# Attention graph units on one core: both column halves of a projection and all values in one round each, 71 rounds a unit

## What is computed

```python
for c in range(6):
    nsrc = min(c + 1, 5); snode = c - nsrc
    eq, ek, ev = lind + nsrc - 1, lind, lind + nsrc // 2
    q = ew[c, 0] * (nodes[c - 1] @ We[eq] + be[eq])
    k = ew[c, 1] * (nodes[snode] @ We[ek] + be[ek])
    v = ew[c, 2] * (nodes[snode + nsrc // 2] @ We[ev] + be[ev])
    o = mha(q, k, v, Wq[c], Wk[c], Wv[c], Wo[c])     # 8 heads of 16, softmax over 1024 keys
    nodes[c] = act_w[c] * o + q
    lind += nsrc
out = layernorm(nodes[5], ln_g, ln_b)
```

## Time and profile before

| what | value |
|---|---|
| median of three runs | 2990.59 us |
| the profiled execution: its time, its span | 2986.32 us, 2984.2 us |
| mean granted TensorE clock | 0.981 |
| TensorE matmul busy | 2845.6 us, 95% of the span |
| VectorE busy | 2396.8 us, 80% |
| ScalarE busy | 2163.1 us, 72% |
| GpSimd busy | 353.2 us, 12% |

### The profile page before, as it was taken

The page is one execution under the profiler, slowest core; times in us unless marked ns, Lnnn a source line. Parts: engine busy times, 40 slices in busy tenths (PEclk is TensorE's granted clock), DMA queues, the critical chain, the costliest instruction groups (busy, mean ns, idle before and its releaser), DMA issues. The chain is left out here.

```text
span 2984.2 us, 49063 instructions
## 1 busy us (share of the span) xinstructions
PE 2845.6 (95%) x18975; PEld 1281.3 (43%) x18975; DVE 2396.8 (80%) x3019; ACT 2163.1 (72%) x2738; POOL 353.2 (12%) x314
## 2 busy tenths in 40 slices
PE   7899999998689999999999999999999999999997
PEld 5566566555333333333333333333333333333332
DVE  6656656665778888888888888888888888888876
ACT  3455655565368888788888888888788888888777
POOL 0000000000001111111111111111111111111011
PEclk7899999999889999999999999999999999999999
DMA  6100000014424544544444534544544434544411
GB/s 149 38 9 12 19 11 14 3 44 80 81 72 84 105 100 96 112 102 88 100 100 96 115 98 84 108 99 96 115 100 87 103 99 94 117 101 92 85 64 40
DMA packets 146190, 239.49 MB, mean 80 GB/s; under 512 B 56802, under 2 KB 97142, under 8 KB 142630
## 3 DMA queue, kind: packets, MB, share of 16 engines
q1 hardware_dynamic: 145958, 236.36, 35.7%
HBM read 162.53 MB, written 70.98 MB: 78 GB/s over the span
## 5 line engine op out<-in xcount | busy, mean ns | idle before, releaser
L1747 ACT ACTIVATE pt_b<-ps_max 128x1024 f32<-128x1024 f32 x1514 | 1487.0, 1025 | 264.7 <-PE ps_max L1566 258.3
L1775 DVE TENSOR_REDUCE mx_b<-ps_pair 128x2 f32<-128x1024 f32 (+1 forms) x989 | 1195.6, 1209 | 176.0 <-PE ps_pair L1554 158.4
L1601 PE MATMUL ps_ctx<-pt_b,vs 128*32 128x512 f32 x6144 | 821.6, 607 | 2.6 <-ACT c_b L1730 2.6
L1775 DVE TENSOR_REDUCE mx_b<-ps_misc 128x1 f32<-128x512 f32 x989 | 673.2, 681 | 64.3 <-PE ps_misc L1554 59.5
L1566 PE MATMUL ps_max<-qs,ks 50*128 50x512 f32 x3028 | 688.9, 429 | 1.6 <-ACT part L1698 0.9
L1554 PE MATMUL ps_pair<-ks,qs 48*128 48x512 f32 x1955 | 490.6, 470 | 28.4 <-DVE mx_b L1775 24.5
L1566 PEld LDWEIGHTS ps_max<-qs,ks 50*128 50x128 f32 x3028 | 321.5, 186 | 257.3 <-ACT pt_b L1747 171.5
L1554 PE MATMUL ps_misc<-ks,qs 48*128 48x512 f32 x989 | 421.0, 426 | 5.0 <-DVE mx_b L1775 1.3
L1554 PEld LDWEIGHTS ps_pair<-ks,qs 48*128 48x128 f32 x1955 | 197.5, 184 | 519.2 <-DVE mx_b L1775 509.0
L931 ACT ACTIVATE pt<-ps_max,cb 128x512 f32<-128x512 f32 x340 | 215.3, 687 | 179.7 <-PE ps_max L658 117.2
L1554 PEld LDWEIGHTS ps_misc<-ks,qs 48*128 48x128 f32 x989 | 183.2, 185 | 212.2 <-DVE mx_b L1775 175.8
(11 more groups left out here) (216 smaller groups left out, 2250.0 us busy)
## 6 DMA issues: line engine op xcount, KB each, us to landing
partd<-part SPq DMA_DIRECT2D x22, 2048.0 KB, 9.1
qs<-partd SPq DMA_DIRECT2D x288, 128.0 KB, 5.6
ks<-partd SPq DMA_DIRECT2D x288, 128.0 KB, 6.6
xv<-node SPq DMA_DIRECT2D x26, 512.0 KB, 5.6
xf<-node SPq DMA_DIRECT2D x24, 512.0 KB, 4.6
xq<-node SPq DMA_DIRECT2D x23, 512.0 KB, 3.8
xk<-node SPq DMA_DIRECT2D x23, 512.0 KB, 4.7
rec_b<-invd SPq DMA_DIRECT2D x368, 32.0 KB, 1.8
```

The source lines that it names most:

```text
L1601: ins = pe.matmul(psO[SLOT * i:SLOT * i + SLOT, :], vs[u % 2][:, kb, QUAD * (s // HALF_STEPS) + i], pt[:, (QUAD * S + i) % ENTRIES], start ...
L1747: act.activation(pt[:, e:e + 2].rearrange("p k n -> p (k n)"), at[:], ACT.Exp, scale=SCALE_B).then_inc(exp_done, 1)
L1775: nc.vector.tensor_reduce(mx2[:, at:at + n], (psP, psX)[p % 2][:, 0:CHUNK * n].rearrange("p (h n) -> p h n", h=n), AX.X, ALU.max).then_inc ...
```

## The change

A project round now makes both halves: two matmuls of 512 columns fill both banks of its tile, and ScalarE copies 1024 columns at a time; there are two such rounds a unit (query, key). One values round makes all eight blocks of values, in both banks, and ScalarE copies them with two instructions. Counters of semaphores follow. `PLAN` has seven entries, so a steady unit has 71 rounds: turn 1 moves from round 6 to 2, the projections stand at 11 and 12 (before 11, 18, 23, 26), output 1 moves from 31 to 23, values stand at 34 (before 34, 39), turn 0 moves from 49 to 44. `PIECE_SLOT` is a new table for 142 slots. Unit 0 now has 70 rounds, so the table holds for units 1 to 21, and units 0 and 22 spread their pieces evenly.

```diff
-        PLAN = {6: ("turn", 0, 1), 9: ("output", -1, 0), 11: ("project", 2, 0), 18: ("project", 2, 1), 23: ("project", 2, 2), 26: ("project", 2, 3),
-                31: ("output", -1, 1), 34: ("values", 1, 0), 39: ("values", 1, 1), 49: ("turn", 1, 0)}
-        FIRST_PLAN = {**PLAN, 0: ("values", 0, 0), 1: ("values", 0, 1)}
+        PLAN = {2: ("turn", 0, 1), 9: ("output", -1, 0), 11: ("project", 2, 0), 12: ("project", 2, 1), 23: ("output", -1, 1),
+                34: ("values", 1, 0), 44: ("turn", 1, 0)}
+        FIRST_PLAN = {**PLAN, 0: ("values", 0, 0)}
...
-        PIECE_SLOT = (1, 2, 4, 7, 8, 10, 12, 14, 17, 18, 18, 19, 19, 24, 25, 27, 29, 30, 32, 33, 34, 36,
+        PIECE_SLOT = (0, 2, 4, 6, 9, 10, 12, 14, 15, 17, 19, 21, 21, 23, 23, 25, 27, 28, 28, 29, 31, 32,
...
-                    pe.matmul(to, wp[:, P * qk:P * qk + P], (xq, xk)[qk][:, CHUNK * c:CHUNK * c + CHUNK],
-                              start=True, stop=True).then_inc(pj_ready, 1)
...
+                    for c in range(NCHUNK):
+                        cols = slice(CHUNK * c, CHUNK * c + CHUNK)
+                        ins = pe.matmul(to[:, cols], wp[:, P * qk:P * qk + P], (xq, xk)[qk][:, cols], start=True, stop=True)
+                    ins.then_inc(pj_ready, 1)
...
+                    for kb in range(KB):
+                        ins = pe.matmul(to[:, P * kb:P * kb + P], xv[:, P * kb:P * kb + P], wv[:],
                                         start=True, stop=True)
...
-                    act.activation(full[:, qk, cols], at, ACT.Identity, bias=wp[:, 2 * P + qk:2 * P + qk + 1])
-                    act.activation(part[:, qk, 0, cols], at, ACT.Identity,
+                    act.activation(full[:, qk], at[:], ACT.Identity, bias=wp[:, 2 * P + qk:2 * P + qk + 1])
+                    act.activation(part[:, qk, 0], at[:], ACT.Identity,
...
-                        ins = act.activation(vs[w % 2][:, BPC * n:BPC * n + BPC, heads, DV * q:DV * q + DV],
-                                             at.rearrange("p (k h d) -> p k h d", k=BPC, h=HEADS)[:, :, heads],
+                        ins = act.activation(vs[w % 2][:, :, heads, DV * q:DV * q + DV],
+                                             at[:].rearrange("p (k h d) -> p k h d", k=KB, h=HEADS)[:, :, heads],
...
-                    pool.wait_ge(pj_copied, PJ * (w - 2) + n + 1)
+                    pool.wait_ge(pj_copied, 2 * (w - 2) + qk + 1)
```

More of the change, by code:

```diff
@@ L1517, in _, with project, values @@
             def _(pe):
-                def project(w, n, to):
-                    qk, c = n // NCHUNK, n % NCHUNK
-                    if n == 0:
+                def project(w, qk, to):
+                    if not qk:
                         pe.wait_ge(p_in, 3 * D16 * (w - 1))
-                    pe.matmul(to, wp[:, P * qk:P * qk + P], (xq, xk)[qk][:, CHUNK * c:CHUNK * c + CHUNK],
-                              start=True, stop=True).then_inc(pj_ready, 1)
-                def values(w, n, to):
-                    if n == 0:
-                        pe.wait_ge(v_in, 2 * D16 * (w + 1))
-                    for t in range(BPC):
-                        kb = BPC * n + t
-                        ins = pe.matmul(to[:, P * t:P * t + P], xv[:, P * kb:P * kb + P], wv[:],
+                    for c in range(NCHUNK):
+                        cols = slice(CHUNK * c, CHUNK * c + CHUNK)
+                        ins = pe.matmul(to[:, cols], wp[:, P * qk:P * qk + P], (xq, xk)[qk][:, cols], start=True, stop=True)
+                    ins.then_inc(pj_ready, 1)
+                def values(w, to):
+                    pe.wait_ge(v_in, 2 * D16 * (w + 1))
+                    for kb in range(KB):
+                        ins = pe.matmul(to[:, P * kb:P * kb + P], xv[:, P * kb:P * kb + P], wv[:],
                                         start=True, stop=True)
@@ L1663, in unit @@
                         elif kind == "values":
-                            values(w, k, to)
+                            values(w, to)
                         elif kind == "project":
-                            project(w, k, to[:, 0:CHUNK])
+                            project(w, k, to)
                         else:
@@ L1689, in _, with project, values @@
             def _(act):
-                def project(w, n, at):
-                    qk, c = n // NCHUNK, n % NCHUNK
-                    act.wait_ge(pj_ready, PJ * (w - 2) + n + 1)
-                    if n == 0 and w > 2:
+                def project(w, qk, at):
+                    act.wait_ge(pj_ready, 2 * (w - 2) + qk + 1)
+                    if not qk and w > 2:
                         act.wait_ge(spilled, D16 * (w - 2))
-                    cols = slice(CHUNK * c, CHUNK * c + CHUNK)
-                    act.activation(full[:, qk, cols], at, ACT.Identity, bias=wp[:, 2 * P + qk:2 * P + qk + 1])
-                    act.activation(part[:, qk, 0, cols], at, ACT.Identity,
+                    act.activation(full[:, qk], at[:], ACT.Identity, bias=wp[:, 2 * P + qk:2 * P + qk + 1])
+                    act.activation(part[:, qk, 0], at[:], ACT.Identity,
                                    bias=wp[:, 2 * P + qk:2 * P + qk + 1]).then_inc(pj_copied, 1)
-                def values(w, n, at):
-                    act.wait_ge(v_ready, 2 * w + n + 1)
+                def values(w, at):
+                    act.wait_ge(v_ready, w + 1)
                     for q in range(2):
                         heads = slice(QUAD * q, QUAD * q + QUAD)
-                        ins = act.activation(vs[w % 2][:, BPC * n:BPC * n + BPC, heads, DV * q:DV * q + DV],
-                                             at.rearrange("p (k h d) -> p k h d", k=BPC, h=HEADS)[:, :, heads],
+                        ins = act.activation(vs[w % 2][:, :, heads, DV * q:DV * q + DV],
+                                             at[:].rearrange("p (k h d) -> p k h d", k=KB, h=HEADS)[:, :, heads],
                                              ACT.Identity)
@@ L1751, in unit @@
                         elif kind == "values":
-                            values(w, k, at[:, 0:CHUNK])
+                            values(w, at)
                         elif kind == "project":
-                            project(w, k, at[:, 0:CHUNK])
+                            project(w, k, at)
                         else:
@@ L1822, in finish_sums @@
                     if k == 4:
-                        dve.wait_ge(v_ready, 2 * UNITS)
+                        dve.wait_ge(v_ready, UNITS)
                     elif k >= PARTS_Y - NCHUNK:
```

12 lines of the change are left out of this document (6 added, 6 removed), and 6 rows, old and new, of the table PIECE_SLOT.

## The result

The changed kernel takes 3057.80 us (median of 4 runs, 3054.96 to 3060.68), the kernel before 2986.02 beside it (4 runs, 2975.85 to 2990.75): a ratio of 1.0243, 95% interval 1.0221 to 1.0264. It is slower by 72 us. The forecast was 3055, slower, with a range of 3005 to 3085.

The account below looks back on a forecast made before the run. TensorE's order with its tile waits was taken as the bound. +3.3 us a unit gave +70 for units 1 to 21, unit 0 -4, unit 22 -1: +65 on 2986.3, 3051; the median's 4.3 made 3055, range 3005 to 3085.

Parts of the forecast that it names:

- Fewer breaks, projections, values: TensorE in a steady unit: four fewer runs -1.2 us, two double projections -0.4, one values round of eight -0.15.
- Tile waits: TensorE waits until VectorE has reduced a maxima tile; in longer runs 8.7 us a unit against 3.6, +5.1.
- P s x P: Run before projection 0: pair of maxima, two score matmuls, misc-tile single, pair; 2.25 us against 1.14, idle 0.9.
- p s x P: Run before the values: pair-tile single, two score matmuls, misc-tile single, pair of maxima; 1.70 us against 1.02.
- the 10: Unbroken run of ten score and maxima matmuls on TensorE: 2.70 us by a hand walk, 2.84 by the row kept.
- the combine: VectorE's combine of the halves at the unit's end, near GpSimd's product: taken at 0, bounds +4 and -7 us in all.
- ScalarE's copies: Eight projection copies of 512 columns (0.69 us each) become four of 1024 (1.02); costed at nothing.
- Moved work: Turn 1 earlier starts SyncE's queue some 4 us sooner, so output 1 at round 23 costs nothing; without it 0.5 us.
- The pair tile's weight-load wait: TensorE's weight load waiting for VectorE's maximum of the pair tile: over 600 us forecast in place of 509.
- (a): Rival: the tile waits don't grow, as VectorE reads sooner or several waits melt into one; 2949 us, chance 0.10.
- (b): Rival: TensorE waits for a bank held by ScalarE's long copies; +42 us on top, 3097, chance 0.05.
- (c): Rival: the waits grow by about the 1.8 us a unit that is gained; 2982 to 3000 us, chance 0.04.

Follow-up runs that it names:

- e1: Changed kernel with one table number changed (19 to 18), moving one pair of maxima ahead of output 0: 3038.2 us, ratio 1.0173.
- e3: Changed kernel, same rounds, with another table of the maxima's places found by walking the unit: 3063.0 us, ratio 1.0257.
- e9: Changed kernel, same 71 rounds and merged copies, with maxima allowed between the halves of projection and values rounds and a table for that: 3012.6 us.
- e8: Kernel before, 74 rounds, with only its table replaced by one from the walk: 3017.5 us, ratio 1.0111.
- e2: Changed kernel with ScalarE's projection copies in halves of 512 columns again, TensorE's order the same: 3058.5 us, ratio 1.0243.
- e10: Changed kernel with turn 1 back at round 6, its old place: 3069.4 us, ratio 1.0278.

## Why the prediction came out right, point by point

**Fewer breaks, projections, values** (-1.75 us): a unit has 38 runs where it had 42, projection 1.92 us (forecast 1.91), values 1.99 (1.96 to 2.16). Confirmed, but for the 0.30 us a break, which is the difference of two shapes and is not measured by itself.

**Tile waits** (+5.1): all runs of an undisturbed middle unit take 50.3 us from start to start, where they took 46.5. That is +3.8; the forecast was +5.1 for waits and -1.2 for breaks, +3.9. Each shape has its price. P s x P 2.25 (forecast 2.25, idle 0.86 against 0.9), p s x P 1.71 (1.70), the 10 2.83 (2.7 to 2.85). e1 takes one of the waits away and moves the kernel by 19.6 us. The unit came to 92.6 against 92.9: 0.1 us of the runs isn't there, and the combine (forecast at nothing) gave back a little. It is long in 17 of the 21 units, where it was in 13, but the context behind it then mostly takes 1.25 us, not 1.55 as before; that is 2 to 3 us in all, inside the bounds of +4 and -7. In the unit shown GpSimd's operation, here the sum, starts 0.37 us ahead of the combine, where the product stood 0.11 ahead, and the combine takes 0.99 us where it took 1.24: in both it ends some 0.1 us behind GpSimd's. The Trainium skill ("SBUF — State Buffer", Who interferes with whom) has the two engines share a port: the trace agrees, as the combines with no operation of GpSimd beside them take 0.22 us. Where GpSimd's starts just behind the combine (0.03 us, unit 4 before) the combine takes 0.22 too.

The walk of the run of 10 has a slip: with the 1.23 and 0.43 us that it names, the pair's reduction ends at 3.41 and the run costs 2.89, not 2.70. Nothing hung on it, as the forecast kept the row's 2.84.

**Why the waits grew** was said, not counted apart: three rounds fewer mean pieces pushed into longer runs. The experiments split the 2.9 us of a unit at full clock. From 92.5 another table for the same rounds goes to 91.5 (e3), places inside the merged rounds with a table for them to 90.4 (e9), 74 rounds with a table of the same making to 90.2 (e8), and the table of the kernel before to 89.6. So 1.1 to 1.3 us hang on the lost places, 1.0 on the table that came with the change, and 0.6 on the table before being better than mine. No run gives the places back under an unchanged table, so the 45 us of e9 are places and table together, with what the clock adds.

**ScalarE's copies** (0): right in effect (e2), off in size. I took 1.02 us for 1024 columns from the Exp, which has no bias tile; the copy with a bias is 1.11. Nothing hung on it, the projections' covers being longer than 2.2 us.

**The sum.** Forecast 21 x 3.3 - 4 - 1 = +65. Measured 21 x 3.0 = +63; unit 0 -1 (from 100.4 to 99.4) and not -4; unit 22 -1; and four units with a clock fall, +9, which no term foresaw. Together +70. The graph stage also starts 2.5 us sooner (820.80 for 823.30) and the last unit is 0.7 longer, and the profiled spans differ by 68.6. So the forecast's total is closer than its parts, and that is luck: 7 us too much for the units stand against 9 too little for the clock and 3 for unit 0. The 3055 has some luck of its own: it is built on 2990.6 for the kernel before, which took 2986.0 beside the changed one, so as a difference 65 was forecast and 72 measured. The step that failed is the silent one, that the unit shown in the earlier trace rows at clock 1.00 stands for all units after the change as well as before.

**Moved work.** Output 1 doesn't wait: GpSimd's sum ends at 1509.8 and TensorE gets there at 1514.24, 33 us behind the unit's first context as forecast. The 0.5 us I'd set against leaving turn 1 at round 6 is right as a warning and off in size: the lead shrinks by some 3.5 us, and two units in 21 wait (e10).

**Signs.** The pair tile's weight-load wait was forecast over 600 us and fell to 319.3. The step behind it took this row as a measure of the path; only starts on the timeline are one. ScalarE's and VectorE's busy time per unit came as forecast (71.4 and 79.3 against 71 and 80).

**Rivals.** (a) fell: the waits didn't melt, in any of the seven shapes looked at. (b) fell by e2, and a score waits on a projection's copy only once, 0.3 us in unit 0. (c) needed growth near 1.8 us, and it was about 5.0 (3.8 and the 1.2 of the breaks).

## What to carry to other kernels

Where one engine's long blocks of work alternate with small pieces that another engine must drain, every break between long blocks is a place for a piece. Before merging rounds to save their entries, count the places that go and price the longer runs by their shape (here 0.30 us a break gained, 0.46 to 1.3 us a run lost); if the merge is wanted for other reasons, keep the places inside it, as e9 does, and make a new table for it. Check the granted clock unit by unit, not by slices of the span, before a difference is put down to waits.
